# A layer of recurrent attention and Hadamard MLP on eight cores: bf16 copies of W1 and W3 made ahead of the MLP

## The reference

```python
xn = layernorm(x)
# attention part: per token, no sum over the sequence
q, k, v = xn @ Wq.T + bq, xn @ Wk.T + bk, xn @ Wv.T + bv      # 16 / 8 / 8 heads of 128
q, k = rope(q), rope(k)
qp, kp = feats(q), feats(k)      # sin and cos of (q/|q|) @ R.T, 128 features
kv = einsum('bhsf,bhsd->bsfd', kp, v)     # kp, v repeated to 16 heads
s = einsum('bhsf,bsfd->bhsd', qp, kv) @ Wo.T + bo
# MLP part, hidden size 8192
hidden = fwht(silu(xn @ W1.T) * (xn @ W3.T))    # Walsh-Hadamard transform
g = silu(hidden @ W2.T)
out = x + s * g
```

## Time and profile before

| | us |
|---|---|
| runs shown | 3421.81 and 3640.81 (median 3531.31) |
| profiled execution | 3437.84 |
| its span, slowest core (core 5) | 3436.3 |
| attention, chunk 0 to the end of chunk 3's mixing | about 0 to 1300 |
| output projection | 1302 to 1430 |
| pass 1: up-projection | 1502 to 1990 |
| pass 1: stage 7 | 2162 to 2397 |
| pass 2: up-projection | 2494 to 2990 |
| pass 2: stage 7 | 3153 to 3416 |

### The profile page before, as it was taken

How to read it: one execution, slowest core, us unless ns; L and a number is a source line. 1 busy time by engine, 2 the same in 40 slices (tenths; PEclk the granted TensorE clock), 3 DMA queues, 4 the chain that set the end, 5 groups by cost and what they waited for, 6 DMA issues and landing times.

```text
span 3436.3 us, 27888 instructions; the slowest of 8 cores (3390.2 to 3436.3 us)
## 1 busy us (share of the span) xinstructions
PE 2135.1 (62%) x9600; PEld 957.4 (28%) x9600; DVE 1158.0 (34%) x3388; ACT 758.9 (22%) x852; POOL 556.0 (16%) x571
## 2 busy tenths in 40 slices
PE   0934353443545008659999933889099999742987
PEld 0322121112212004424444410334044444301433
DVE  2145874685587891111111114010311111140011
ACT  4253135115313112332222200000422222200000
POOL 0212460452245341000000000000000000000000
PEclk9966665666667558879999965899599999956977
DMA  6575826937541101157777876453378787676442
GB/s 136 98 123 89 132 31 117 135 61 115 75 80 25 25 0 35 59 104 148 155 149 149 163 143 161 169 172 135 97 134 161 141 152 152 151 139 196 149 156 110
DMA packets 131019, 405.63 MB, mean 118 GB/s; under 512 B 10560, under 2 KB 92480, under 8 KB 96576
## 3 DMA queue, kind: packets, MB, share of 16 engines
q0 software_dynamic: 38080, 294.79, 45.4%
q1 hardware_dynamic: 50432, 75.50, 7.3%
q10 hardware_dynamic: 42368, 33.56, 4.0%
HBM read 589.55 MB, written 75.50 MB: 194 GB/s over the span
## 4 chain that ended last, share of the span: by engine, by line
PE 47%; DMA 21%; DVE 10%; ACT 8%; POOL 8%; issue 4%; ACTq 1%; DVEq 0%; POOLq 0%; SPq 0%
PE p L1201 13%; PE p L989 9%; DMA W3A<-W3T 9%; PE p L994 9%; PE p L371 7%; DMA U<-S 4%; PE p L835 3%; DMA XBa<-XBAT 3%; POOL PSCR L767 3%; DVE TMP L747 3%; DVE U L1088 3%; POOL PSCR L769 2%; PE p L429 2%; DMA S<-U 2%; POOL PSCR L772 1%
## 5 line engine op out<-in xcount | busy, mean ns | idle before, releaser
L1015 DVE TENSOR_TENSOR U<-GT,p 128x512 bf16<-128x512 bf16 x128 | 88.1, 688 | 849.3 <-ACT GT L1007 849.3
L1007 ACT ACT_TABLE_LOAD x128 | 164.2, 1283 | 777.4 <-PE p L994 766.8
L1201 PE MATMUL p<-WA,U 128*128 128x512 bf16 x1024 | 247.3, 404 | 139.2 <-DMA U<-S 122.3
L989 PE MATMUL p<-XNT,WA 128*128 128x512 bf16 x1024 | 250.0, 401 | 79.9 <-DMA W3A<-W3T 63.9
L641 PE MATMUL pT<-IDENTs,SBf 128*128 128x128 bf16 x128 | 16.2, 305 | 441.8 <-POOL SBf L777 297.8
L747 DVE SCALAR_TENSOR_TENSOR TMP<-QP,KP 128x128 bf16<-128x128 bf16 x1024 | 228.4, 287 | 113.9 <-POOL SBf L777 86.7
L1201 PE MATMUL p<-WB,U 128*128 128x512 bf16 x1024 | 242.0, 398 | 4.9 <-DMA WB<-W2Bd 4.9
L989 PE MATMUL p<-XNT,WB 128*128 128x512 bf16 x1024 | 231.4, 379 | 8.6 <-DMA W3B<-W3T 8.6
L994 PE MATMUL p<-XNT,W3A 128*128 128x512 bf16 x1024 | 231.5, 379 | 0.0
L994 PE MATMUL p<-XNT,W3B 128*128 128x512 bf16 x1024 | 231.4, 379 | 0.0
L1233 DVE TENSOR_TENSOR TMPR<-SBf,GT 128x512 bf16<-128x512 bf16 x32 | 13.6, 425 | 616.1 <-ACT GT L1216 612.8
(11 more groups left out here) (158 smaller groups left out, 2780.2 us busy)
## 6 DMA issues: line engine op xcount, KB each, us to landing
W2Bd<-W2T POOLq DMA_DIRECT2D x32, 1024.0 KB, 34.1
WA<-W1T POOLq DMA_DIRECT2D x32, 1024.0 KB, 9.2
W3A<-W3T POOLq DMA_DIRECT2D x32, 1024.0 KB, 15.1
WB<-W1T POOLq DMA_DIRECT2D x32, 1024.0 KB, 9.7
W3B<-W3T POOLq DMA_DIRECT2D x32, 1024.0 KB, 14.7
WA<-W2Bd POOLq DMA_DIRECT2D x32, 1024.0 KB, 5.1
WB<-W2Bd POOLq DMA_DIRECT2D x32, 1024.0 KB, 5.2
XBa<-XBAT SPq DMA_DIRECT2D x8, 1024.0 KB, 15.7
```

What stands on the lines that cost most here:

```text
L989: last = t.matmul(pu[:, :t_chunk], b1[:, k * 256 + al * 128: k * 256 + (al + 1) * 128], XNT[:, k * t_chunk:(k + 1) * t_chunk], start=(k == ...
L1007: upt[("silu", a_)] = tk.inc(a.activation(GT[:, (a_ % 2) * 512:(a_ % 2) * 512 + t_chunk], pu[:, :t_chunk], AF.Silu), "ac")
L1015: upt[("gate", a_)] = tk.inc(v.tensor_tensor(U[:, a_ * t_chunk:(a_ + 1) * t_chunk], GT[:, (a_ % 2) * 512:(a_ % 2) * 512 + t_chunk], pl_[:, ...
L1201: last = t.matmul(bank[:, :], U[:, a_ * t_chunk + ts * 128: a_ * t_chunk + (ts + 1) * 128], buf[:, al * 1024 + dc * 512: al * 1024 + (dc + ...
```

## The change

Two HBM tensors W1Bd and W3Bd are added. The cast list now holds the 32 pieces of W1, then the 32 of W3, then the 32 of W2. In attention chunks 1 to 3 each job issues up to four casts, until 64 have been issued, that is all of W1 and W3. The up-projection loads W1Bd and W3Bd in place of W1T and W3T, in both passes, and each block of pass 1 issues one cast of W2 behind its two loads. The line of the wait in `p5g` is unchanged; what `tk.tok("dwe")` gives there changes, since casts are issued between blocks. The device computes the same values.

```diff
--- before.py
+++ after.py
@@ -89,6 +89,8 @@
     SIND = nc.dram_tensor("SINS", [t_batch, 128], F32, kind="ExternalInput")
     S1 = nc.dram_tensor("S1", [FF, t_chunk], BF16)
     S2 = nc.dram_tensor("S2", [FF, t_chunk], BF16)
+    W1Bd = nc.dram_tensor("W1Bd", [32, 128, NDT * 256], BF16)
+    W3Bd = nc.dram_tensor("W3Bd", [32, 128, NDT * 256], BF16)
     W2Bd = nc.dram_tensor("W2Bd", [32, 128, 4 * 1024], BF16)
 
     dbg = {}
@@ -322,12 +324,14 @@
             + [(WKT, BKs, KB, oc) for oc in range(2)]
             + [(WVT, BVs, VB, oc) for oc in range(2)])
 
-    cast_list = [(W2Bd, W2T, j) for j in range(32)]
+    cast_list = [(wd, ws, j)
+                 for ws, wd in ((W1T, W1Bd), (W3T, W3Bd), (W2T, W2Bd))
+                 for j in range(32)]
     cast_ptr = [0]
 
-    def emit_casts(g, kmax=2):
+    def emit_casts(g, kmax=6, limit=96):
         for _ in range(kmax):
-            if cast_ptr[0] >= len(cast_list):
+            if cast_ptr[0] >= min(len(cast_list), limit):
                 return
             wd, ws, j = cast_list[cast_ptr[0]]
             cast_ptr[0] += 1
@@ -349,7 +353,7 @@
             ), sem, 16)
             evt[("w", ji)] = tk.tok(sem)
             if c > 0:
-                emit_casts(g)
+                emit_casts(g, kmax=4, limit=64)
         blk.gpsimd(p1g)
 
     def emit_p1t(blk, c, ji):
@@ -964,15 +968,16 @@
                     tk.wait(g, "pl", wcons[s1_], tk.tok("dwe"))
                     tk.inc(g.dma_start(
                         bass.AP(b1, 0, [[8192, 128], [1, 4096]]),
-                        bass.AP(W1T, gb * 128 * 4096, [[4096, 128], [1, 4096]]),
+                        bass.AP(W1Bd, gb * 128 * 4096, [[4096, 128], [1, 4096]]),
                     ), s1_, 16)
                     upt[("w1", gb)] = tk.tok(s1_)
                     tk.wait(g, "pl", wcons[s3_])
                     tk.inc(g.dma_start(
                         bass.AP(b3, 0, [[4096, 128], [1, 4096]]),
-                        bass.AP(W3T, gb * 128 * 4096, [[4096, 128], [1, 4096]]),
+                        bass.AP(W3Bd, gb * 128 * 4096, [[4096, 128], [1, 4096]]),
                     ), s3_, 16)
                     upt[("w3", gb)] = tk.tok(s3_)
+                    emit_casts(g, kmax=1)
                 blk.gpsimd(p5g)
 
                 for al in range(2):
```

## The result

The change makes the kernel 0.7% slower: the ratio of its time to that of before, measured side by side on the same chips, is 1.007 (95% interval 1.0053 to 1.0087), some 24 us (20.6 us between the two profiled executions, as the table below has it). That is inside the 2% which count as no change here, and the interval lies above 1. The profiled execution took 3451.16 us (span 3449.5, core 0). The forecast was 3471 us and +33 us against its base. The median of 3531.31 us shown for before was the middle of an undisturbed run and one with one die at a lower clock; the comparisons leave out such runs and, in experiment 1, the cores of such a die.

What follows compares the result with a forecast made beforehand. The chain ran through PE for 47% of the span and DMA for 21%. 3437.8 + 28 (X tiles) + 7 (POOL's issues) + 35 (pass 1) - 37 (pass 2) gave 3471 us, range 3395 to 3540.

Steps and rivals of the forecast that it cites:

- so the chain of casts sets the period: Pass 1: W1, W3, cast and S1 writes in order take 16.8 us a block, over PE's 14.24; +43 us.
- the 5.6 us and twice 1.7 us left for DVE and the slow starts: Pass 2: this part of the 38 us excess was held unrelated to loads and would stay, leaving -29 us.
- the base: The profiled execution of the kernel before, 3437.84 us, to which the terms were added.
- The X tiles: Attention chunks 1 to 3: XBb lands 8, 10 and 10 us late beside the longer cast burst; +28 us, bounds +3 and +42.
- POOL's issues: Attention chunks: two more cast issues, 0.98 us each time, ahead of POOL's products; +7 us, bounds 0 and +16.
- The chain's sum: Pass 1, from W1's issue to the cast's landing: 5.1 + 3.0 + 8.0 + 0.7 = 16.8 us.
- The low end of 5.0 us: Lowest cast price, from the burst at 403 us; pass 1 would then be PE-bound and gain, -42 us.
- rivals 1 and 4: Rival 1: casts hidden in pass 1, 3399 us, 0.16. Rival 4: only bytes count, casts free, 3350 us, 0.07.
- Rival 2: Pass 1: slower chain of casts, 9.2 us a cast, period 18.0 us, 3509 us, or 3540 with slower loads; chance 0.14.
- the upper bound given: Pass 2: all the excess goes, with the first load's gain; -46 us.
- rival 3: Chunks 1 and 2: queue full, PE waits for V weights, 30 us more in each; 3531 us, chance 0.13.

Runs made afterwards that it cites:

- experiment 1: The changed kernel with POOL waiting for the casts only before the first W1 load of pass 1; lowest time 3442.97 us, the changed kernel's 3440.95.
- experiment 6: The changed kernel with the casts of jobs 3 to 5 of each chunk issued behind POOL's products instead of ahead; ratio to before 1.0091.
- experiment 4: The kernel before with 64 casts instead of 32 in attention chunks 1 to 3, the further ones copying W1 unread; ratio to before 1.0146.
- experiment 5: The changed kernel with no casts behind the first two weight loads of a chunk and more behind each of the others; lowest time 3544.72 us.
- experiments 2: Changed kernel, no cast wait inside pass 1, second cast per block: period 26.1 us; or W2 cast early, bf16 copy per block: period 14.23 us.
- experiment 3: The changed kernel with all W2 casts before pass 1, 27 in chunk 4 and five behind the last Wo load; lowest time 3457.48 us.
- experiment 7: Against the kernel before: casts respread, 26 in last chunk and output projection, bf16 copies for 15 blocks in pass 1, 20 in pass 2; ratio 0.9769.

## Why the forecast was right, and where it was wrong

**What missed.** The forecast was 3471 us, the profiled execution took 3451: the slowest core's span grew by 13 us and not by 33. The touched parts give +31, the untouched rows -10, and the slowest core of before stood 17.6 us above the mean of its eight, that of after 10.2. Three steps failed: in pass 1 "so the chain of casts sets the period", since the bytes that two cores share set it; in pass 2 the 5.6 us and twice 1.7 us left for DVE and the slow starts, of which nothing stayed; and the base, a slow last stage 7.

**Attention, the sum right, its parts not quite.** Forecast +35 us, measured +36. The X tiles, forecast +28, are 35.0 us of longer ACT waits in the mean of the cores: XBb, the tile that the forecast named, 22.0, and XBa, taken to land as before, 12.9. That leaves 1 us for POOL's issues, forecast +7, and experiment 6 did not find them either. So two errors made up for each other. That the casts alone do this is shown (experiment 4), and for chunk 1 that it goes through the X tiles (experiment 5).

**Pass 1, the number right and its cause mostly wrong.** Forecast +35 us; measured +47.8 up to the last W1 load and -7.2 behind it, +41. The period was 17.07 us for 16.8. The chain is there, and releases the loads. But the step "so the chain of casts sets the period" fell: without the wait a block still took 16.62 of the 17.07 us. The wait is worth 20 us up to the last W1 load and 11 with the row behind it; the rest is that 5.51 MB of HBM traffic a block don't pass at more than 331 GB/s a core. The chain's sum was near by luck. The forecast had 5.1 (W1) + 3.0 (W3) + 8.0 (cast) + 0.7; the table's trace has 7.4 + 2.9 + 6.1 + 0.6. W1 took 2.3 us more and the cast landed 1.9 us sooner behind W3. That this is the neighbour's traffic beside W1 was not tried. What one more cast adds, where nothing waits for it, is 9.5 to 9.6 us (experiments 2 and 3), more than the 8.0. The low end of 5.0 us, and with it rivals 1 and 4, rested on a moment in which the neighbour core was quiet; a look at that core's window would have ruled them out ahead of the run. Rival 2's price of a cast, 9.2, was near that, and its sum of 18.0 too high, since in the measured chain the cast landed 6.1 us behind W3.

**Pass 2, right in kind, too small.** Forecast -37 us, measured -46 (42.7 + 2.9), the upper bound given. The step that failed is "I leave 5.6 us for the waits on DVE (L1015)" with the slow starts behind them, said to have nothing to do with loads. After the change none is left. What had misled was the releaser's name: PE had waited for the DMA. The earlier trace rows has at 1593.90 us in before a wait of 2.70 us put down to DVE. The DMA issue of before at that block, issued at 1577.59:

```profile
W3A<-W3T POOLq DMA_DIRECT2D x1, 1024.0 KB, 16.1
```

It landed at 1593.66 us, and PE began at 1593.90; DVE's product ended at 1593.66 too, so this row alone can't tell the two apart. The same goes for the waits of pass 2: W3A landed at 2587.09, PE began at 2587.33. The trace after the change can. There PE starts on a block 2.6 us before DVE's product of the block before it is ready:

```profile
2690.76 3.62 PE L994 MATMUL p<-XNT,WB 128*128 128x512 bf16 x16
...
2692.69 0.69 DVE L1020 TENSOR_TENSOR U<-GT,p 128x512 bf16<-128x512 bf16 x1 [6.22 <-ACT GT L1012]
```

So these matmuls don't need that product, and the 9 us belonged to the loads, too.

**The base.** 3437.8 us was an execution whose two slowest cores lost some 20 us in the last stage 7, where the change has no part. The parts that the change touches sum to 36 + 41 - 46 = +31 us (forecast +33), while the mean cores of the two profiled executions differ by 21 us, 10 us of it in the table's first and last row. The ratio over several runs, +24 us, lies between. Added to the low runs of before (3414 to 3429) the forecast's +33 would have given 3447 to 3462; the changed kernel took 3441 to 3451.

**The queue (rival 3), not here, but near.** No PE wait for V weights came. In pieces of 1.049 MB, chunk 1 or 2 reads 24 for its weights and 4 for X, and its 24 casts move 72: 105 MB, at 331 GB/s an estimated 317 us, as long as the chunk itself (313.5). Experiment 5 shows how little it takes to turn this into 40 us a chunk.

**Open.** Single profiles of one code differ: experiment 3, whose chunks 1 to 3 are the change's, took 322, 316 and 315 us there, cores from 310.9 to 324.4 in chunk 3. So the 5 us or so by which experiments 4 and 6 lie above the change in chunk 3 are not read. That the pair of cores is what shares the 331 GB/s rests on stretches in which one core happened to be quiet; a run in which only one core of each pair casts was not made. Experiment 7 changes several things at once, and how much each of them gives is told by the rows and not by runs of their own.

## What to carry to other kernels

A copy in HBM is paid in bytes of the memory that two cores share: count what it reads and what it writes, for both cores at once, and look at the neighbour's window before taking a cheap transfer as the price. Moving such work is free only where the memory idles (26 casts in experiment 7), and even there it must not stand in front of a load that somebody waits for soon (27 casts in experiment 3, 85.6 us). When the profile names one releaser of a wait for several, look at the landing of the DMA as well. Copy only as many blocks as the idle stretches pay for, rather than all of them.

## What the runs showed of the hardware

- A cast of 2 MB to 1 MB in HBM cost 9.5 us (pass 1) and 9.6 us (a burst of 27) with both cores of a pair casting, and 5.0 us beside a quiet neighbour (19 bursts of the trace before).
- The DMA engines' busy share rose from 0.78 to 0.99 while the rate stayed at 200 to 202 GB/s: the share tells that packets are under way, not that bytes move. The rate counts destination bytes, 235 GB/s with a copy of equal types against 202 with the cast.
- One core alone reached 210 GB/s of cast output (630 of HBM), two together 222 (666).
